# Tree stage of a two-layer Perceiver kernel: ScalarE takes the leaves first, VectorE's decisions wait for the logits alone

## The reference, cut to what matters

```python
logits = x @ W_in.T + b_in
decisions = (logits > 0).astype(jnp.int32).reshape(B, PAR, N_NODES)
acts = jax.nn.silu(logits).reshape(B, PAR, N_NODES)
current = jnp.zeros((B, PAR), dtype=jnp.int32)
dmap = jax.nn.one_hot(current, N_NODES, dtype=acts.dtype)
for d in range(DEPTH):
    moves = jnp.take_along_axis(decisions, current[..., None], axis=2)[..., 0]
    current = (current - (2 ** d - 1)) * 2 + moves + 2 ** (d + 1) - 1
    dmap = dmap + jax.nn.one_hot(current, N_NODES, dtype=acts.dtype)
out = (acts * dmap).reshape(B, WIDTH) @ W_out.T
```

## Time and profile before

| | |
|---|---|
| median of three runs | 2155.56 us |
| time of the profiled execution | 2140.7 us |
| its span, first to last instruction | 2138.9 us |
| PE busy | 1901.4 us (89%) |
| DVE busy | 1400.1 us (65%) |
| ACT busy | 1256.8 us (59%) |
| mean granted TensorE clock | 0.952 |
| tree stage, first logits to last add | 1981.1 to 2134.6 us |

### The profile page before, as it was taken

The page is one execution under the profiler, slowest core; times in us unless marked ns, Lnnn a source line. Parts: engine busy times, 40 slices in busy tenths (PEclk is TensorE's granted clock), DMA queues, the critical chain, the costliest instruction groups (busy, mean ns, idle before and its releaser), DMA issues. The chain is left out here.

```text
span 2138.9 us, 65491 instructions
## 1 busy us (share of the span) xinstructions
PE 1901.4 (89%) x28518; PEld 1190.4 (56%) x28528; DVE 1400.1 (65%) x2413; ACT 1256.8 (59%) x1783; POOL 248.4 (12%) x279
## 2 busy tenths in 40 slices
PE   8899999999998586999699999999999997757888
PEld 5577777777755453333356566565666655445333
DVE  3677777777636655555578888887887884455444
ACT  3477777777733552222278778777777876355222
POOL 4000000000031511111001001001001100041000
PEclk8999999999999687999799999999999999869999
DMA  4455545544300200111644544554554450120110
GB/s 141 107 134 131 130 132 132 140 123 126 74 3 10 52 4 23 40 36 30 131 84 84 94 84 92 93 89 94 88 93 94 84 77 8 15 49 3 39 30 30
DMA packets 63929, 161.63 MB, mean 76 GB/s; under 512 B 21796, under 2 KB 26020, under 8 KB 63268
## 3 DMA queue, kind: packets, MB, share of 16 engines
q1 hardware_dynamic: 61828, 154.33, 33.7%
q10 hardware_dynamic: 1824, 3.20, 0.7%
HBM read 68.13 MB, written 1.05 MB: 32 GB/s over the span
## 5 line engine op out<-in xcount | busy, mean ns | idle before, releaser
L603 ACT ACTIVATE Pb<-ps 128x1024 f32<-128x1024 f32 (+2 forms) x640 | 634.2, 1002 | 206.6 <-PE ps L552 158.4
L675 DVE TENSOR_REDUCE MX<-ps 128x2 f32<-128x804 f32 (+1 forms) x386 | 368.8, 986 | 59.9 <-PE ps L519 58.7
L572 PE MATMUL ps<-Pb,V 128*17 128x64 f32 (+1 forms) x13312 | 360.0, 248 | 9.0 <-issue 4.1
L677 DVE TENSOR_REDUCE MX<-ps 128x1 f32<-128x402 f32 (+1 forms) x512 | 278.0, 571 | 101.4 <-PE ps L523 91.6
L572 PEld LDWEIGHTS ps<-Pb,V 128*17 128x17 f32 (+1 forms) x13312 | 256.3, 97 | 96.0 <-issue 63.4
L519 PE MATMUL ps<-KST,QW 50*128 50x402 bf16 (+1 forms) x1024 | 176.6, 340 | 24.0 <-ACT V L622 17.2
L552 PE MATMUL ps<-QW,KST 50*128 50x128 bf16 (+1 forms) x3328 | 165.5, 219 | 30.0 <-ACT Pb L603 29.4
L503 PE MATMUL ps<-W,CT 128*128 128x128 f32 (+1 forms) x1144 | 168.1, 286 | 1.1 <-ACT V L622 1.1
L552 PEld LDWEIGHTS ps<-QW,KST 50*128 50x128 bf16 (+1 forms) x3328 | 101.0, 96 | 113.2 <-ACT Pb L603 84.0
L495 PE MATMUL ps<-CT,W 128*128 128x402 f32 (+1 forms) x352 | 146.6, 541 | 18.5 <-DMA CT<-ctxT 12.0
L523 PE MATMUL ps<-KST,QW 96*128 96x402 bf16 (+1 forms) x512 | 154.1, 339 | 4.8 <-issue 2.2
(11 more groups left out here) (232 smaller groups left out, 2697.8 us busy)
## 6 DMA issues: line engine op xcount, KB each, us to landing
CT<-ctxT SPq DMA_DIRECT2D x44, 800.5 KB, 5.0
KST<-HL SPq DMA_DIRECT2D x320, 100.1 KB, 3.0
KST<-C SPq DMA_DIRECT2D x320, 100.1 KB, 3.0
ABO<-ctxT SPq DMA_DIRECT2D x10, 800.5 KB, 5.5
T<-ctxT SPq DMA_DIRECT2D x10, 800.5 KB, 4.4
KST<-HL SPq DMA_DIRECT2D x128, 50.0 KB, 2.7
KST<-C SPq DMA_DIRECT2D x128, 50.0 KB, 2.7
CT<-experts SPq DMA_DIRECT2D x32, 192.0 KB, 2.3
```

What stands on the lines that cost most here:

```text
L572: mm = nc.tensor.matmul(ps[32 * quad:32 * quad + m, SUM, oc:oc + nh * S], V[0:n, b % 2, tile, v0:v0 + m], Pb[0:n, buffer(b, x), ti * att.W ...
L603: nc.scalar.activation(Pb[0:n, buffer(b, x), 0:banks * 512].rearrange("p (a c) -> p a c", a=banks), score_banks(b, x)[0:n, 0:banks, :], AC ...
L675: nc.vector.reduce_max(MX[:, b % 2, 2 * j:2 * j + 2], work(job)[:, :, 0:n], AX.X).then_inc(freed["dve"], 1)
L677: nc.vector.reduce_max(MX[:, b % 2, j:j + 1], work(job)[:, 0:n], AX.X).then_inc(freed["dve"], 1)
```

## The change

ACT's two activations change places: the leaves' first. The inner nodes' activation now waits for `dec`, and both raise `acts`, which counts two for a unit. DVE's decisions wait for `log` in place of `acts`; its masks wait for `path` and then for `acts` at 2n + 2. No instruction is added or removed except waits, and PE's and SP's lists are as they were.

```diff
                     eng.wait_ge(s["log"], n + 1)
                     if sweep or not (isinstance(tree, int) and tree == 0):
                         eng.wait_ge(s["down"], n - 1)
-                    nc.scalar.activation(Pb[0:INNER, cc, 0:CH], ps[0:INNER, 2 + cc, :], ACT.Silu,
-                                         bias=biases(slot, 0, INNER))
                     nc.scalar.activation(Pb[:, cc, CH:2 * CH], ps[:, 4 + cc, :], ACT.Silu, bias=biases(slot, 1, 128)
                                          ).then_inc(s["acts"], 1)
+                    eng.wait_ge(s["dec"], n + 1)
+                    nc.scalar.activation(Pb[0:INNER, cc, 0:CH], ps[0:INNER, 2 + cc, :], ACT.Silu,
+                                         bias=biases(slot, 0, INNER)).then_inc(s["acts"], 1)
 
             def dve_tree(sweep, tree, slot):
                 for cc in range(2):
                     n = unit(sweep, tree, cc)
 
-                    eng.wait_ge(s["acts"], n + 1)
+                    eng.wait_ge(s["log"], n + 1)
                     nc.vector.tensor_scalar(DEC[0:INNER, cc, :], ps[0:INNER, 2 + cc, :], biases(slot, 0, INNER), 0.0,
                                             ALU.add, ALU.is_gt).then_inc(s["dec"], 1)
                     eng.wait_ge(s["path"], n + 1)
+                    eng.wait_ge(s["acts"], 2 * n + 2)
                     for k, rows, thr in ((0, INNER, "thr0"), (1, 128, "thr1")):
```

## The result

The changed kernel's median was 2117.23 us (four runs, 2114.77 to 2120.18) against 2152.77 us before (four runs), a ratio of 0.9858 with a 95% interval from 0.9823 to 0.9893. The change makes the kernel faster, and by more than I had forecast: 2117 lies under my range of 2125 to 2147.

The account below looks back on a forecast made before the run. The chain through ACT was taken to bound the kernel, then PE: 1.30 + 1.88 + 1.35 + 0.05 + 29 x 0.587 = 21.6 us off the 2155.6 us median, giving 2134 us, range 2125 to 2147.

Parts of the forecast that it names:

- Steady period: Tree stage, paths to paths: 3.92 us instead of 4.507, summed from PE's starts; gain 0.587 us in each of 29 periods.
- the bound of 3.97: Steady period if the two bf16 path products take 0.48 us instead of 0.43; 1.4 us less gain in all.
- the rival of drained passes: PE drains the fp32 passes before the first path product; a period gains 0.38 us, total 2140 us; chance 0.10.
- Start of the stage: Unit 0: paths wait for the decisions alone, which move from 1984.42 to 1983.12; gain 1.30 us.
- Sweep change: Between the sweeps, 8.00 us: ACT's 1.30 go and 0.05 of the first path product; gain 1.35 us.
- Tail: After the last paths: nothing changes but 0.05 us; masks, down, add and store stay.
- Unit 1: Second unit of the stage, 5.80 us before: period 3.92, gain 1.88 if PE's clock holds; gain 0.19 if it falls.
- up to 0.05 us late, not on PE's order, which does logits first: Unit 0: inner activation ends 1.51 us after the logits, paths 1.49; the lateness was taken not to delay PE.
- ACT and DVE reading PSUM at once: Simultaneous reads from separate banks: 3% of 1.44 us, 0.04 us, inside the cover.
- The moved wait: Rival: masks wait for the inner activation, against 0.68 us of cover after it in steady units; 2153 us, chance 0.04.
- The clock: PE's clock at unit 1 holds, 6 to 4; total gain 19.9 us if it falls. Slower-clock rival: 1.2 GHz, 0.03.
- nothing in the stage scales with that difference, so I take the same microseconds off the median: From profiled execution (2140.7 us) to median: the same 21.6 us come off 2155.6, giving 2134 us.

Follow-up runs that it names:

- experiment 7: Kernel before with the leaves' down product (line 1621) left out; period 4.51 us, single run 2146.71 us.
- experiment 8: Changed kernel with the leaves' down product (line 1621) left out; period 3.21 or 3.22 us in 28 of 31 intervals, single run 2106.51 us.
- experiment 6: Changed kernel with two more 128x512 activations on ACT ahead of the leaves' one; periods alternate 3.93 and 4.24 us, single run 2135.07 us.
- experiment 1: Kernel before, unedited, timed against itself; ratio 1.000 (0.9977 to 1.0023), 12 runs around a median of 2152.4 us.
- experiment 3: Kernel before with 64 added waits that are always met already; ratio 0.9997 (0.9976 to 1.0018), stage 158.1 us.
- experiment 5: Kernel before with the leaves' activation moved ahead of the inner one, decisions still waiting for both; periods 4.50 and 4.51 us, single run 2137.66 us.
- experiment 4: Changed kernel with the decisions waiting for the leaves' activation instead of the logits; ratio 0.9904 (0.987 to 0.9939), period 3.97 us on the mean.
- experiment 2: Changed kernel, unedited, repeated; ratio 0.9900 (0.9874 to 0.9926), median 2130.6 us.
- experiment 10: Changed kernel, unedited, timed a third time; ratio 0.9908 (0.9881 to 0.9936), median 2124.6 us.

## Why the prediction was right or wrong

**The mechanism was right, and the stage's gain came to 0.6 us of the forecast.** Step by step:

- *Steady period*: 3.92 forecast, 3.92 measured. PE binds (experiments 7 and 8). The bf16 products start one fp32 pass after the last one, with their weights loaded under it, so the bound of 3.97 and the rival of drained passes (4.13) are out.
- *Start of the stage*: first logits to first paths 4.10 before, 2.80 after (1976.17 to 1978.97), 1.30 as forecast. *Sweep change*: 8.00 to 6.64, 1.36 (forecast 1.35). *Tail*: 0.05.
- *Unit 1*: forecast 3.92, measured 4.41. The clock held, as forecast, but the step by which the inner activation is "up to 0.05 us late, not on PE's order, which does logits first" was mis-sized. It ended at 1979.64, and DVE began the masks 0.45 later, so the down products were late; at unit 16 the same hand-over took 0.10, and unit 17 took 4.05. The two units came out 0.49 and 0.13 us longer than 3.92.
- Sum: 1.30 + 1.39 + 14 x 0.586 + 1.36 + 0.46 + 14 x 0.586 + 0.05 = 21.0 us, which is what the traces have from the first logits to the end of the last add (153.5 to 132.5). The forecast was 21.6. The missing 0.6 are in units 1 and 17, and not all of it is the late hand-over: 0.10 is that of the two path products in units 0 and 16, where PE does wait. They are 0.26 apart there (1978.97 and 1979.23), and the sum took 0.22 for every pair.
- *ACT and DVE reading PSUM at once* costs nothing that these rows show. The groups of the changed kernel in the stage, with busy time and mean ns:

```profile
L1655 DVE TENSOR_SCALAR DEC<-ps,CT 127x512 bf16<-127x512 f32 x32 | 24.0, 751 | 12.2 <-PE ps L1606 12.2
...
L1644 ACT ACTIVATE Pb<-ps,CT 128x512 f32<-128x512 f32 x32 | 22.0, 687 | 82.6 <-PE ps L1606 82.6
```

  Both start together, from different banks, in all units but unit 1, where DVE comes 0.05 us later from its late masks, and take the 0.75 and 0.69 us of before. The Trainium skill (PSUM — Partial Sum Buffer, Specifications (TRN2)) says that the two read in parallel at full bandwidth unless they meet in one bank; the trace agrees. What a meeting in one bank would do, which the new wait for `dec` excludes, no run here shows.
- *The moved wait* didn't come: 0.68 us of cover, confirmed by experiment 6. *The clock* held instead of falling: in the seven profiles of kernels with the short chain it is 1.00 throughout the stage's two sweeps; in the five with the long one (the first profile, experiments 1, 3, 5 and 7) it falls one to three times. Where the kernel before falls differs by profile, so the 1.3 us that the sum took off unit 1 stand for this one profile; in experiments 1 and 3 there would be 1.7 us at the sweep change in their place.

**What failed is the step from the stage to the median.** I wrote "nothing in the stage scales with that difference, so I take the same microseconds off the median" and set the range by three runs. The time of a run is the stage's time plus the moment at which it begins. The stage repeats: 136.8 us in three profiles of the changed kernel, and 157.8, 158.15 and 158.1 in the two of the kernel before and in experiment 3. (Experiment 5, with the same period, took 163.0 by two more falls of the clock, so a run of the kernel before may have more than its profiles show.) The moment at which it begins varies on its own: in the twelve profiles the first logits came between 1972.9 (experiment 5) and 1993.2 (experiment 4), for kernels that are the same up to there.

The mean granted clock goes with it: 0.957 and 0.956 in the two earliest, 0.946 and 0.950 in the two latest. An estimate from windows of 4 us over the first 1968 us, each counted as 8 x (1 - granted clock) us at the lower level: 171 us at 1.2 GHz in the earliest (experiment 5), 185 in the first profile of the changed kernel, 198 in that of the kernel before, 222 in experiment 1. Over the twelve, the correlation of this time with the start is 0.78. The first profile of the changed kernel has 13 us less of it than that of the kernel before, which is up to 6.7 us of PE's work at half speed and enough for the 5.0 us by which it began earlier. So the clock in stages that the change doesn't touch accounts for much of the spread; no run held it fixed to show the rest.

The four first runs of the changed kernel had spans of 2113.0 to 2118.3; less a stage of 136.8 us, their first logits lay at about 1976 to 1981.5, in the early part of that spread, and so 35.5 us came out where the stage gives 21. The forecast of 2134 was 16.7 too high: 2.8 because a fourth run took the median before from 2155.6 to 2152.8, 13.9 because 35.5 us came off and not 21.6. The lower end of the range was set by three runs that reached 8.6 under their median; the twelve of experiment 1 reach 11.6 under theirs. The two repetitions gave 20.5 us (2151.1 - 2130.6) and 20.8 us (2145.5 - 2124.6), with medians of which one lies inside the forecast range and one 0.4 us under its lower end.

**What stays open**: the first four runs of the changed kernel (2114.8 to 2120.2) all lie under the six of experiment 2. Part of it is the clock: in the twelve runs of experiments 2 and 10 a mean clock lower by 0.001 goes with about 1.2 us more (correlation -0.82), and the first four had 0.953 on the mean where those twelve had 0.949. That makes about 5 of the 10.5 us between the two means. Why the clock was higher, and the rest, the runs don't tell: chance, or the chip (the kernel before had medians of 2151.1 and 2145.5 us on two of them). Only one run of the kernel before was made beside those four (2149.99).

**The chances**: 0.57 for within 1% and 0.40 for faster. The stage's own gain is 21.0 of 2152 us, 0.98%, on the line as forecast; the first measurement fell beyond it, the repetitions on it (0.9900) and within (0.9908).

## What to carry to other kernels

When a unit on the chain is taken off, don't count its length but what the next engine has left: 1.28 us of ACT were worth 0.59 in a period, because PE's own work filled 3.92 of 4.51, and 0.72 of them could be put back for 0.05. PE's bound is best summed from starts of matmuls that follow each other without a wait, here or in another stage, not from the modelled ends or the idle time (0.37) that the page books. And read the gain from the stage in the trace: where the rest of the kernel varies by 20 us from run to run, a median over four runs can be off by two thirds of what the change is worth (14 us on 21 here), and a forecast range has to allow for it.

## What the runs showed of the hardware that was not expected

- The clock's fall goes with the idle time that a chain leaves to PE at the start of a sweep, and it moves: with waits of 2.14 us at the stage's start and 1.50 and 2.14 at the sweep change it fell at the first (5.80), at the second (9.69), or at both and in unit 17 too (experiments 5 and 7), for 1.3 to 1.7 us each. With the waits for the decisions cut from 2.14 to 0.84 us (1.56 in experiment 4) it did so in none of seven profiles. An idle time of 1.23 us in every steady unit (experiment 7) brought no fall in any of them. So here the shorter chain paid twice.
- The hand-over from ACT to DVE, for masks that wait for two semaphores and get ACT's last, takes 0.10 us (experiments 4, 6 and 8 and unit 16), where the decisions with a single one start 0.02 to 0.04 after ACT. Whether that is the second wait or the other kind of instruction, no run separates. In the first unit of the stage it takes 0.45, in all seven profiles with the short chain (1979.64 to 1980.09 in the first). Experiment 6 shows that it isn't the paths: ACT ends at 1994.50 there, 0.9 us after the paths are through, and the masks still start at 1994.95. Why it takes so long was not tried.
